# Attention and expert layer on one core: the sums of the exponentials come from a column of ones beside the values, and ScalarE takes two of a batch's eight distance copies

## The reference, cut to what matters

```python
def _L0_attn_ref(q, Wq, bq, Wk, bk, Wv, bv, Wo, bo, rel_table):
    Q = (q @ Wq + bq).reshape(b, s, h, d).transpose(0, 2, 1, 3)      # K, V alike
    scores = jnp.einsum('bhid,bhjd->bhij', Q, K) / jnp.sqrt(d)
    rel_idx = jnp.clip(pos[None, :] - pos[:, None] + MAX_REL, 0, 2 * MAX_REL)
    scores = scores + jnp.einsum('bhid,ijd->bhij', Q, rel_table[rel_idx])
    attn = jax.nn.softmax(scores, axis=-1)
    ctx = jnp.einsum('bhij,bhjd->bhid', attn, V).transpose(0, 2, 1, 3).reshape(b, s, e)
    return ctx @ Wo + bo
...
    h = _layernorm(x, axis=-1) * (1 + ca) + sa
    x = x + ga * _L0_attn_ref(h, ...)          # ga: one row of 128 gains for each batch
    h = _layernorm(x, axis=-1) * (1 + cb) + sb
    x = x + gb * _L0_ffn_ref(h, ...)           # router, top 2 of 8 experts, silu, sum
```

## Time and profile before

| what | value |
|---|---|
| time, median of 3 runs | 687.17 us (685.5 to 690.84) |
| the profiled execution: its own time | 685.29 us |
| the profiled execution: span | 683.6 us |
| busy in the span | PE 588.5, ACT 508.8, DVE 507.1, POOL 423.3 us |
| granted TensorE clock, mean over the span | 0.96 |

### The profile page before, as it was taken

One profiled execution on the slowest core, in us unless ns is written; L12 is line 12 of the kernel. 1 busy time (PEld: TensorE's weight loads), 2 busy tenths in 40 slices (PEclk: granted clock), 3 DMA queues, 4 the chain that ended last, 5 costly groups with the idle time before them and its releaser, 6 DMA issues. The chain is left out here.

```text
span 683.6 us, 17706 instructions
## 1 busy us (share of the span) xinstructions
PE 588.5 (86%) x5108; PEld 439.8 (64%) x5108; DVE 507.1 (74%) x1888; ACT 508.8 (74%) x1578; POOL 423.3 (62%) x543
## 2 busy tenths in 40 slices
PE   5667789999899899899989989978798989999950
PEld 4444556666666566566666656655577979999940
DVE  6788988999999999999999999997565312222127
ACT  4157799999999999999989999998643434444434
POOL 2660655747668687686776966855366765554535
PEclk9777999999999999999999999999999999999975
DMA  5996678778787788778868878874525777565538
GB/s 142 308 230 202 198 235 248 228 235 248 214 245 241 213 252 246 228 219 260 249 208 242 252 213 247 243 236 148 189 82 174 236 234 228 198 217 185 176 97 274
DMA packets 173125, 149.03 MB, mean 218 GB/s; under 512 B 16182, under 2 KB 162642, under 8 KB 173030
## 3 DMA queue, kind: packets, MB, share of 16 engines
q1 hardware_dynamic: 168054, 139.33, 67.9%
q0 software_dynamic: 4544, 8.44, 3.7%
q10 hardware_dynamic: 432, 0.14, 0.1%
HBM read 83.71 MB, written 65.05 MB: 218 GB/s over the span
## 5 line engine op out<-in xcount | busy, mean ns | idle before, releaser
L711 ACT ACTIVATE P<-NS,nmax 128x256 f32<-128x256 f32 x512 | 254.2, 504 | 50.5 <-DVE nmax L1312 49.6
L1312 DVE CUSTOM_DVE_ANT_0 NS<-psS,bias 128x256 f32<-128x256 f32 x512 | 185.2, 417 | 2.3 <-PE psS L950 1.6
L968 PE MATMUL psT<-ident,P 128*128 128x128 f32 x1024 | 140.0, 281 | 8.9 <-ACT PT L722 8.8
L1267 DVE COPY stage<-psDist 128x768 f32<-128x768 f32 x125 | 118.1, 945 | 33.9 <-issue 25.2
L722 ACT ACTIVATE PT<-psT 128x512 f32<-128x512 f32 x256 | 136.4, 586 | 0.0
L968 PEld LDWEIGHTS psT<-ident,P 128*128 128x128 f32 x1024 | 118.2, 145 | 24.0 <-issue 9.8
L778 ACT ACTIVATE F<-psS,b1T 128x256 f32<-128x256 f32 x156 | 65.4, 471 | 86.5 <-PE psS L1061 86.5
L609 POOL DMA_INDIRECT results_d<-y,row_u x78 | 76.0, 974 | 56.7 <-DVE y L1458 40.8
L711 ACT ACTIVATION_READ_ACCUMULATOR P<-NS,nmax 128x1 f32 x512 | 100.3, 196 | 0.0
L950 PE MATMUL psS<-Kst,Qst 32*128 32x256 f32 x512 | 65.9, 336 | 34.7 <-DVE nmax L1312 29.9
L1061 PE MATMUL psS<-xT,w 128*128 128x256 f32 x312 | 80.6, 381 | 0.3 <-DMA w<-in_L_ffn_w_dram 0.3
(11 more groups left out here) (254 smaller groups left out, 1044.2 us busy)
## 6 DMA issues: line engine op xcount, KB each, us to landing
dist_d<-stage SPq DMA_DIRECT2D x128, 384.0 KB, 3.0
bias<-dist_d SPq DMA_DIRECT2D x256, 192.0 KB, 3.3
w<-in_L_ffn_w_dram SPq DMA_DIRECT2D x39, 512.0 KB, 3.7
x<-slots_d SPq DMA_DIRECT2D x39, 129.0 KB, 3.0
y<-results_d SPq DMA_DIRECT2D x16, 256.0 KB, 5.0
dist_d<-zeros SPq DMA_DIRECT2D x1, 2048.0 KB, 14.4
out_dram<-y SPq DMA_DIRECT2D x8, 256.0 KB, 3.2
results_d<-y,row_u POOLq DMA_INDIRECT x78, 3.0
```

Of the source, the lines that this page charges most:

```text
L711: act.activation(P[:, p % 2, h, q, :], NS[:, p % 2, h, q, :], ACT.Exp, scale=-1.0, bias=nmax[:, p % 2, k:k + 1], accum_out=lsum[:, b % 2, ...
L968: mm = pe.transpose(psT[:, h, S * k + 128 * q:S * k + 128 * q + 128], P[:, p % 2, h, q, 128 * k:128 * k + 128], ident[:])
L1267: dve.tensor_copy(stage[:, p % STAGES, :, :, :], bank[:, :, 0:2 * RW].rearrange("p h (q c) -> p h q c", q=2)).then_inc(dist_out, 1)
L1312: dve.tensor_tensor_reduce(NS[:, p % 2, h, q, :], psS[:, h, S * q:S * q + S], bias[:, p, h, q, :], 1.0, 3e38, ALU.add, ALU.min, nmax[:, p ...
```

## The change

The values get two heads of 16 columns for each group of 32 rows of `psO`: eight values, a one, and seven zeros. The product that weighs the values so also gives the row sums, in both halves of `psO`. `accum_out`, `lsum`, `inverses`, `widen` and `spread_l` go. ACT copies all 512 columns of `psO` out at the start of step 3 (`copy_values`), PE turns them back with four transposes in step 3 (`turn_values`), so that tokens are on the partitions, and DVE inverts the sums and multiplies in step 4 (`context`, one step later than before, a reciprocal and a product). PE turns the context with two transposes in step 4 (job "ct", in the place of "y"), ACT copies it, and the product with the output weights becomes the extra job "y" of step 6: for each of two halves of tokens one product with weights that hold the gains (`WoG`) and one that adds the bias row. The gained weights are made for each batch in step 7 (extra job "gain": one product on PE, one multiplication on DVE), from two rows turned once (job "gains"). Of the distance copies, those of steps 0 and 4 go from DVE to ACT, behind `gather`, from batch 1 on. The output weights and the values' bias come in the needed order from the host's arrays, so SP loads each with one transfer.

```diff
+BY_ACT_OUT = (0, 4)
...
-           (("y", -1), ("nh", 2)), (("u01", -2),), (("u23", -2),), (("q01", 2),))
-X_SLOTS = ((), (("rank", -4),), (("turn", -2),), (("back", -2),), (("tally", 1 - B),), (("rows", -3),), (("t", -1),), ())
+           (("ct", -1), ("nh", 2)), (("u01", -2),), (("u23", -2),), (("q01", 2),))
+X_SLOTS = ((), (("rank", -4),), (("turn", -2),), (("back", -2),), (("gains", 0), ("tally", 1 - B)), (("rows", -3),),
+           (("y", -1),), (("gain", 0),))
...
+def act_puts_out(b, p):
+
+    return b > 0 and p in BY_ACT_OUT and PAIRS * b + p + AHEAD < STEPS
...
-            for a in range(4):
-                at = slice(32 * a, 32 * a + 32)
-                sp.dma_start(WoD[at, :], Wo.rearrange("(g a d) e -> a g d e", a=4, d=D)[a]).then_inc(weights_in, 16)
-                sp.dma_start(bvT[at, :], bv.rearrange("(g a d x) -> a g d x", a=4, d=D, x=1)[a],
-                             allow_slow_non_contiguous=True).then_inc(weights_in, 16)
+            sp.dma_start(WoD[:], Wo).then_inc(weights_in, 16)
+            sp.dma_start(bvT[:], bv.rearrange("(e a) -> e a", a=1)).then_inc(weights_in, 16)
...
-            def widen(b):
-                pool.wait_ge(linv_done, b + 1)
...
-                                   bias=nmax[:, p % 2, k:k + 1],
-                                   accum_out=lsum[:, b % 2, q, a, p // 2:p // 2 + 1]).then_inc(exp_done, 1)
+                                   bias=nmax[:, p % 2, k:k + 1]).then_inc(exp_done, 1)
...
-                    i = act.activation(yT[:], bank[:, 0:S], ACT.Identity, scale=modT[:, 2, b:b + 1],
-                                       bias=gabo[:, b:b + 1])
+                    i = act.activation(ctxT[:], bank[:, 0:S], ACT.Copy)
...
-            def sums(b):
-                act.wait_ge(ctx_full, b + 1)
-                past(act, ctx_done, b)
-                act.activation(lrow[:], psO[:, S:2 * S], ACT.Copy).then_inc(lrow_done, 1)
+            def copy_values(b):
+                act.wait_ge(values_done, HG * b + HG)
+                past(act, ctx_full, b)
+                act.activation(C[:], psO[:], ACT.Copy).then_inc(c_copied, 1)
+
+            def put_out(n):
+                act.wait_ge(dist_done, n + 1)
+                act.wait_ge(written[(n - STAGES) % SLOTS], 16 * ((n - STAGES) // SLOTS) + 16)
+                act.activation(stage[:, n % STAGES, :, :, :],
+                               psD[:, :, 0:2 * RW].rearrange("p h (q c) -> p h q c", q=2), ACT.Copy)\
+                    .then_inc(dist_out, 1)
...
                 if (b, p) > (0, 0):
                     gather(*at)
+                if act_puts_out(b, p):
+                    past(act, x_dve, X_DONE[b, p][1])
+                    past(act, x_act, X_DONE[b, p][2])
+                    put_out(PAIRS * b + p + AHEAD)
...
-                elif name == "y":
+                elif name == "ct":
                     pe.wait_ge(ctx_done, b + 1)
-                    mm = pe.matmul(bank[:, 0:S], WoD[:], ctxT[:], start=True, stop=True)
+                    for k in range(2):
+                        mm = pe.transpose(bank[:, 128 * k:128 * k + 128], ctx_r[:, k, :], ident[:])
...
-                elif name == "t":
-                    pe.wait_ge(m_act, M_TAKEN["y", r][1])
+                elif name == "y":
+                    pe.wait_ge(m_act, M_TAKEN["ct", r][1])
+                    pe.wait_ge(x_dve, X_TAKEN["gain", r][0])
                     for k in range(2):
-                        mm = pe.transpose(spare[:, k, :], yT[:, 128 * k:128 * k + 128], ident[:])
+                        pe.matmul(spare[:, k, :], ctxT[:, 128 * k:128 * k + 128], WoG[:], start=True, stop=False)
+                        mm = pe.matmul(spare[:, k, :], ident[:, r:r + 1].broadcast_to([128, 128]), gR[:, 1, :],
+                                       start=False, stop=True)
...
+                elif name == "gain":
+                    mm = pe.matmul(spare[:, 0, :], ident[:, r:r + 1].broadcast_to([128, 128]), gR[:, 0, :],
+                                   start=True, stop=True)
...
-            def spread_l(b):
-                pe.wait_ge(linv_wide, b + 1)
+            def turn_values(b):
+                pe.wait_ge(c_copied, b + 1)
                 for q in range(2):
-                    mm = pe.transpose(psO[:, S + 128 * q:S + 128 * q + 128],
-                                      linvD[:, q, :, :, :].rearrange("p a g d -> p (a g d)"), ident[:])
+                    for r in range(2):
+                        mm = pe.transpose(psO[:, S * q + 128 * r:S * q + 128 * r + 128],
+                                          C[:, S * r + 128 * q:S * r + 128 * q + 128], ident[:])
                 mm.then_inc(ctx_full, 1)
...
-                    if p == 2:
-                        spread_l(b - 1)
+                if p == 3 and b > 0:
+                    turn_values(b - 1)
...
+            for g in range(HG):
+                i = dve.memset(V[:, :, :, g, :, g % 2, D:D + 1].rearrange("p b k a d -> p (b k) (a d)"), 1.0)
+            i.then_inc(ones_in, 1)
...
-            def inverses(b):
...
             def context(b):
-                dve.wait_ge(lrow_done, b + 1)
+                values = psO[:].rearrange("p (n m d) -> p n m d", n=4, d=2 * D)
+                dve.wait_ge(ctx_full, b + 1)
+                dve.reciprocal(linv[:], values[:, :, :, D:D + 1].rearrange("p n m d -> p n (m d)")).then_inc(linv_done, 1)
                 if b > 0:
-                    dve.wait_ge(m_full, M_FULL["y", b - 1])
-                dve.tensor_tensor(ctxT[:], psO[:, 0:S], lrow[:], ALU.mult).then_inc(ctx_done, 1)
+                    dve.wait_ge(m_full, M_FULL["ct", b - 1])
+                dve.wait_ge(linv_done, b + 1)
+                dve.tensor_tensor(ctx_r[:].rearrange("p q (r m d) -> p (q r) m d", r=2, d=D), values[:, :, :, 0:D],
+                                  rep(linv[:], 3, D), ALU.mult).then_inc(ctx_done, 1)
...
-                if p == 0 and b > 0:
-                    inverses(b - 1)
...
-                if p == 3 and b > 0:
+                if p == 4 and b > 0:
                     context(b - 1)
...
-                if n < STEPS:
+                if n < STEPS and not act_puts_out(b, p):
                     past(dve, x_full, so_far(X_DONE, b, p)[0])
                     put_out(n, psD)
```

More of the change, by code:

```diff
@@ L56 @@
 X_LATE = ()
-BY_ACT = ("y", "nh", "back")
-M_LAST = (("logits", B - 3), ("y", B - 1), ("u01", B - 2), ("u23", B - 2), ("logits", B - 2), ("u01", B - 1),
+BY_ACT = ("ct", "nh", "back")
+M_LAST = (("logits", B - 3), ("ct", B - 1), ("u01", B - 2), ("u23", B - 2), ("logits", B - 2), ("u01", B - 1),
           ("u23", B - 1), ("logits", B - 1))
-X_LAST = (("turn", B - 2), ("rows", B - 3), ("t", B - 1), ("back", B - 2), ("turn", B - 1), ("rank", B - 3),
+X_LAST = (("turn", B - 2), ("rows", B - 3), ("y", B - 1), ("back", B - 2), ("turn", B - 1), ("rank", B - 3),
           ("rows", B - 2), ("back", B - 1), ("rows", B - 1), ("rank", B - 1))
@@ L803, in _ @@
             act.activation(p1[:, 0:1], ident[:, 0:1], ACT.Silu)
-            sums(B - 1)
-            act.wait_ge(m_full, M_FULL["y", B - 1])
-            take("y", B - 1, banks[1])
+            copy_values(B - 1)
+            act.wait_ge(m_full, M_FULL["ct", B - 1])
+            take("ct", B - 1, banks[1])
             units(0, 1)
```

70 lines of the change are left out of this document (34 added, 36 removed).

## The result

The changed kernel takes **699.92 us** (median of 4 runs, 697.5 to 701.36), the kernel before 686.34 beside it on the same chip (4 runs, 683.55 to 690.84): a ratio of **1.0188, interval 1.0124 to 1.0252**, slower by more than the 1% that a measurement can tell. The forecast was 699. The profiled execution took 699.25 with a span of 697.5, 13.9 more than the span before.

The account below looks back on a forecast made before the run. PE was taken to set the pace in steps 3 to 5. 14 x (0.75 + 0.2) = 13.3 plus 7 x (0.31 - 0.15) = 1.1, less 2.0 and 0.5, gave +11.9 on the median 687.17: 699 us, range 686 to 707.

Parts of the forecast that it names:

- Steps 3 and 4: PE waits 0.7 to 0.9 us at step 4's weighing for DVE's late context; step 5's scores come 0.75 later.
- Rival 2: The context is in time, so the weighing's wait vanishes: 688.6 us; chance 0.22.
- Plain batches: Batches without routing: 0.75 delay, 0.2 gain and 0.31 output product, less 0.15 relief; 1.11 us longer each.
- The gain: DVE's multiplication for the gained weights, ahead of step 0's extremes, costs 0.2 us in every batch.
- The output product: Four fp32 products replace two transposes on PE: 0.31 us more in a plain batch, nothing in a routing one.
- relief in step 0: DVE loses a reciprocal and one copy in step 0: 0.15 us back in plain batches, nothing in routing ones.
- Routing batches: Batches with routing work: 0.75 delay and 0.2 gain, output product and relief at nothing; 0.95 us longer each.
- ACT's relief: ACT comes out some 1.5 us lighter per batch, 2.9 of it saved accumulators; costed at nothing, PE's queue covering it.
- Rival 3: ACT's copies come late by 0.7 in both steps and hold PE's scores, 14 x 1.4: about 719 us; chance 0.07.
- Rival 1: ACT, the fullest engine, sets the pace, so the change is faster: about 664 us; chance 0.13.
- The start: Fewer load issues on SP let the zeros start 4.4 us earlier, shortening DVE's wait for distances: 2.0 us off.
- The end: Shorter last exponentials on ACT against a longer last output product: 0.5 us off.

Follow-up runs that it names:

- experiment 1: The changed kernel with DVE's context of step 4 put ahead of the takes of router product and values: 691.82 us, ratio 1.0113 to the kernel before.
- experiment 8: Experiment 5's kernel with the gained weights made only once, in batch 0: 682.78 us, ratio 0.9976.
- experiment 7: Experiment 5's kernel without the two products that add the bias row to the attention's output: 684.04 us, ratio 0.9967.
- experiment 5: Experiment 1's kernel with DVE's `chosen` moved ahead of step 6's copy of the distances: 687.2 us, ratio 1.0029.
- Experiment 2: The kernel before without the accumulation of row sums in the exponentials (softmax left undivided): 689.73 us, ratio 1.0079.
- experiment 4: The changed kernel with all distance copies on DVE again, none on ACT: 700.13 us, ratio 1.0229.
- experiment 6: The kernel before without the accumulation of row sums, and with `chosen` moved ahead of step 6's distance copy: 682.26 us, ratio 0.9957.
- experiment 3: The kernel before with output weights and values' bias loaded by one transfer each: 683.57 us, ratio 0.9979.
- experiment 10: The kernel before with one-transfer loads of output weights and bias, and batch 0's gates ahead of step 2's copy on DVE: 680.53 us, ratio 0.9900.
- experiment 9: Experiment 5's kernel with step 0's copy on DVE where a rank product follows, and batch 0's gates ahead of step 2's copy: 681.5 us, ratio 0.9908.

## Why the prediction came out right, and where its steps were wrong

**Steps 3 and 4, right in place, and a little small in size.** The forecast's wait at the weighing, 0.7 to 0.9, stands in the trace as 0.75, and taking it away gave back 0.75 in a plain and 0.65 in a routing batch (experiment 1). It is 10.1 of the 13.9 us. The delay of step 5's scores, which the forecast took as 0.75 (0.64 to 0.84), is 0.93 (7.47 for 6.54), 0.09 over its bound; 0.16 of it stays in experiment 1 (6.70 from 269.18 to 275.88). Rival 2, the context in time, is what experiment 1 built; it took 691.82 and not the rival's 688.6, and the six long `chosen` were still in it.

**Plain batches, right in sum, partly by luck.** The gain cost 0.19 (experiment 8; forecast 0.20). The output product costs 0.89 from its start at 255.75 to the next turn at 256.64, 0.23 over the 0.66 of the earlier trace rows; the forecast took 0.31. What remains of the 1.10 is 1.10 less 0.93, 0.19 and 0.23, that is -0.25, beside the forecast's -0.15 of relief in step 0. A delay 0.18 too small stands against an output product 0.08 too large and a relief 0.10 too small, so that 1.10 meets 1.11.

**Routing batches, the terms that failed.** "In a routing batch it lies beside DVE's `choose` operations" held for PE's products (experiment 7: nothing). But the gain's "0.2 in every batch" was wrong there (experiment 8: nothing in five periods of six), and the cost that is there was in no term: `chosen` at 1.10 in the place of 0.21, 0.73 of a routing batch (experiment 5). The other unforeseen cost is the last period's, 2.38, with its lower clock; "its clock is no term here" was read in plain batches (1.00) and does not hold there (0.84 for 0.94). And the first routing period grew by 2.12 and the four behind it by 1.44 to 1.47, and only in these four the kernel before had a long `ahead_of` to lose (what that one cost was not tried by itself). The forecast costed ACT's relief at nothing "since PE's queue covers it" and looked for what would uncover it only on PE's side. It did not ask what a lighter ACT would start earlier: POOL's product, into an instruction of DVE. Experiment 2 shows that this alone does it, in a kernel without the rest of the change. The relief itself was over-sized: the accumulators are worth 2.3 us of ACT and not 2.9, and ACT came out 1.0 lighter in a plain batch and not 1.5.

**Rival 3, in one place.** ACT's copies hold PE, but not the scores, and not by 1.4: the rank product waits 0.29 in a routing batch and 1.35 in the last one. Taken over all batches the copies on ACT are worth about nothing (experiment 4).

**Rival 1.** ACT was the fullest engine and did not set the pace: 2.3 us less of it moved a plain batch by 0.44 (experiment 2). The rule that the forecast quoted from the Trainium skill, "Perfetto Trace Analysis", section "Identifying the Most-Contended Engine", to work first on the engine with the highest occupancy, names ACT here. Lightening ACT made the kernel 4.3 us slower (experiment 2), and 3.5 faster once `chosen` was moved (experiment 6), where the rival had 21 for 1.5 us a batch: the measurement decides against the rule here.

**The start, mis-sized: -6.5 for -2.0.** The loads are worth the 2.0 (experiment 3: 1.8). Another 3.1 is step 2 of batch 0, 5.45 in the changed kernel's profile and 8.54 before. Of that, 1.3 is DVE's wait for distances that came late at the lower clock, and most of the rest is the gates, which then met POOL's split (tenth experiment); in the changed kernel they missed it, and only their last instruction was held, by another product (0.66 at 40.86). This is not the change's doing: experiments 4 and 7 have the changed kernel's start and took 8.52 and 8.54 there, experiment 2 has the old start and took 5.45. What decides which clock a profile has there, and what lies behind the last 1.6, was not tried.

**The end.** +2.3 where -0.5 was forecast, but kernels with the same code behind batch 15's mark took 207.4 (before), 209.5 (experiment 3) and 212.0 (experiment 10) in their profiles. One profile each can't price this stretch to better than some 5 us, and the row says nothing of the change.

So the mechanism was right where its largest term lies, and the total was right by luck beside it: two misses of the sum, 4.6 too little in the routing batches and 4.5 too little off in the start, happened to cancel; the end's 2.8 and the plain batches' 0.9 make the remaining 2.0 of the span. The change itself, mended (experiment 9), stands where the kernel before stands with the mends that do not need it (experiment 10): 0.9908 and 0.9900.

## What to carry to other kernels

Moving a step later in one engine's program costs what its last consumer then waits, where that consumer's engine sets the pace, and that can be read off the two timelines ahead of time, to 0.2 us here. When an engine off the critical path is made lighter, follow what it releases: its consumers start earlier, and a small instruction of another engine may now start behind a long one with which it shares a resource. Small instructions whose durations jump (0.2 to 1.1 here) show it in a profile. Moving one of them by one place gave back some 0.75 us of a routing batch, where taking 2.3 us off the fullest engine gave back 0.44 of a plain one. And a profile is one execution: compare the granted clock of a stretch before its length is put down to an edit.

## What the runs showed of the hardware

- A DVE instruction on operands in SBUF that starts behind a POOL tensor instruction ended 0.02 to 0.09 us after that one's end, in the pairs of rows above (0.21 became 1.10, 0.17 became 0.96). Started 0.11 ahead of POOL's, it took its usual 0.21 and POOL's 1.27 was no longer either. DVE's extremes, which read PSUM and one operand in SBUF, showed no such stretch (none of the changed kernel's 512 took over 0.42). The longer `ahead_of` ended 0.27 after POOL's product, and POOL's copy behind it took 0.60 for 0.39, so either engine can be held.
- It hits also an instruction with one tensor in SBUF and a scalar from SBUF (the gates' last, 1.12 for 0.23).
- An exponential without its accumulator starts 0.40 after the one ahead and not 0.49, and the saving is 2.3 us of ACT's busy time in a plain batch.
- The granted clock is not the same in the same stretch of two profiles: 0.56 and 1.00 in step 2 of batch 0, where eight transposes took 1.86 (39.79 before) and 1.04 (36.08 after).
- A wait for several semaphores was put down to ACT's `PT` in all 10.7 us of the weighing's idle time, though moving DVE's context alone removed it.
